# A state-space mixer kept channel-major: decay rows by DMA, diagonal and state products turned round, gate and squares channel-major

## The chip, the cores and the metric

The kernel runs on one core of one Trainium2 chip. The metric is the time of one execution on the device in microseconds; the time before is the median of three runs, 2385.97 us (2383.77 to 2386.37).

The engines are named as in the profile: PE multiplies matrices (PEld loads its weights), DVE, ACT and POOL work element by element, SP issues most DMAs. Each runs its own instructions in order and waits on semaphores. Operands lie in SBUF, PE writes to eight PSUM banks of 2 KB a partition.

## The reference

Layer norm and a mixer of Mamba-2 kind on 2 x 512 tokens of width 512, then layer norm and a mixture of experts, a block-sparse projection and the experts again, each added to x. The change touches the mixer alone. It has 8 groups of 16 heads with 64 channels, state size 128; the kernel takes chunks of 128 tokens where the reference has 32, for the same result.

```python
zxbcdt = hidden_states @ in_proj_w.T              # gate, x, B, C, dt
xBC = silu(causal_conv4(xBC) + conv_b)
dt = softplus(dt + dt_bias);  xs = x * dt;  Adt = -exp(A_log) * dt
A_cumsum = cumsum(Adt)                            # inside a chunk
L = exp(segment_sum(Ac))                          # exp(c_i - c_j), i >= j
Y_diag = einsum('bhcij,bcjhd->bcihd', (C @ B.T) * L, xs)
states = einsum('bckhn,bhck,bckhd->bchdn', B, exp(A_last - A_cumsum), xs)
# states are carried from chunk to chunk with exp(A_last)
Y_off = einsum('bckhn,bchdn,bhck->bckhd', C, states, exp(A_cumsum))
y = Y_diag + Y_off + D * x
y = y * silu(gate)
y = y * rsqrt(mean(y*y over the group's 1024 channels) + EPS) * norm_w
out = y @ out_proj_w.T
```

## The kernel before

After the first layer norm and the preparation (dt, the running sums c of A dt, and from them tables by token) a loop runs 8 times, once a group. Its body is one list of steps k, the same on every engine, unrolled: in step k each engine's code holds `if` blocks for all that is due in k. A unit of the recurrence is a pair of heads (128 channels) of one batch, four chunks of 128 tokens: 16 units u, unit u = (pair, batch).

- k 0 to 19: projection and convolution of B, C and the 8 tiles of x, for each batch. PE: 12 matmuls (weights and data are each split in a high and a low part, three products, helper `three`, L1479) into bank k % 3. ACT writes the last tap (L845), DVE adds the other three (L1164), ACT takes a tanh (L858), and DVE (k up to 9, L1173) or POOL (L641, L644) completes silu. x is channel-major here, [channel, token], in a ring of four buffers `cv`.
- k 20 to 35: 16 gate units of 12 matmuls: token-major, for tokens t and half of the channels. Tanh on ACT (L886), product on DVE (L1234), multiplied into Y on POOL (L654), squares summed on ACT (L900).
- k 36 to 43: 8 output tiles of 24 matmuls. Before each half, PE transposes y back to channel-major (`y_transpose`, L1526), ACT and DVE split it in parts `ah` (L915) and `al` (L1253). DVE adds the tile, times the reciprocal root rs8, to X (L1248). ACT's square root (L904) is in step NORM_AT = 38.

The recurrence of unit u runs beside these steps, at offsets `T_X, A_, B_, C_, D_ = 8, 9, 10, 11, 11`:

- k = u+8: PE transposes x to token-major (L1622) into bank TR.
- k = u+9: ACT copies it to Y (L808); DVE makes xs = x dt (L1225) and POOL xd = x dt decay (L610) from Y. PE spreads the two heads' rows c over the partitions with a matmul each (L1579: `pick_head` picks three bf16 parts from `rows`), ACT takes relu(c_j - c_i) (L874).
- k = u+10: ACT exponentiates (L815), DVE multiplies by G = C B (L1211). PE makes the state products of three chunks (L1594), DVE carries them along (L1147, L1152: S).
- k = u+11: PE makes the diagonal part in bank 6 (L1636) and the off part (L1650: weights C, columns S). DVE adds D x and the diagonal part (L1185) and scales the off part into yo (L1199).
- k = u+12: POOL adds yo to Y (L636).

State and off products share bank 7, so L1650 of unit u waits for the S of unit u+1. ACT and POOL also split the weights into `wh` (L826) and `wl` (L620), at the steps of `W_TICK`; SP loads them as the ring `raw` of four gets free.

## Time and profile before

| | |
|---|---|
| Median of 3 runs | 2385.97 us |
| Profiled execution | 2383.2 us, its span 2381.5 us |
| Mean granted TensorE clock | 0.975 of 2.4 GHz |
| PE, DVE, ACT, POOL busy | 92%, 68%, 51%, 44% of the span |
| HBM read and written | 142.42 MB and 25.95 MB |

"Span" is from the first instruction to the last. Groups of instructions are told apart by line, tiles and shape, and their "mean ns" is of one instruction; neighbours on one engine overlap by some 0.07 us, so that what follows starts a little before the end printed. A matmul's printed duration includes its way through the array: the distance of the starts is what it costs in a row of matmuls. fp32 matmuls have two records each. A wait stands in brackets behind the instruction that had to wait.

### The profile page before, as it was taken

The numbers are of one execution on the slowest core, as the hardware profiler recorded it, in microseconds if no ns is written. First come the engines' busy times: TensorE is split into PE (matmuls) and PEld (weight loads), VectorE is DVE, ScalarE is ACT, GpSimd is POOL, SyncE is SP. The second block draws the span as 40 slices with busy tenths as digits, with TensorE's granted clock in tenths as the row PEclk, the third lists the DMA queues.
The fourth block names the chain that finished last, engine by engine and source line by source line (L and its number), as shares of the span: only waits on it lengthen the run. The fifth ranks groups of instructions, "written<-read, shape, count | busy, mean of one in ns | idle before, by whom it ended". The sixth has DMA issues, their size and how long they took to land.

```text
span 2381.5 us, 40261 instructions
## 1 busy us (share of the span) xinstructions
PE 2201.0 (92%) x12416; PEld 1827.9 (77%) x12416; DVE 1630.3 (68%) x2891; ACT 1217.8 (51%) x2809; POOL 1051.3 (44%) x882
## 2 busy tenths in 40 slices
PE   3899999999999999999999999899989988989897
PEld 2778877887788778878887888788878867766775
DVE  6797389739973997499649965985598553157314
ACT  2576366636663665266537653764376422422341
POOL 3476047505750575057416731673276213430322
PEclk7999999999999999999999999999999999999999
DMA  1201011111011011101110111001101027950795
GB/s 60 100 28 36 20 44 32 32 35 32 28 32 40 27 32 33 40 23 37 41 29 26 36 37 31 31 28 37 35 28 27 18 97 250 391 168 36 261 398 159
DMA packets 87218, 171.26 MB, mean 72 GB/s; under 512 B 11464, under 2 KB 11464, under 8 KB 86984
## 3 DMA queue, kind: packets, MB, share of 16 engines
q1 hardware_dynamic: 78016, 140.35, 17.6%
q0 software_dynamic: 7520, 24.65, 3.2%
q10 hardware_dynamic: 1448, 3.41, 0.4%
q8 instruction: 114, 1.87, 0.3%
q14 instruction: 120, 0.98, 0.1%
HBM read 142.42 MB, written 25.95 MB: 71 GB/s over the span
## 4 chain that ended last, share of the span: by engine, by line
PE 55%; DVE 23%; issue 15%; POOL 3%; ACT 3%; DVEq 1%; another core or an unknown queue 1%; DMA 0%; ACTq 0%; POOLq 0%; SPq 0%
PE bank L1479 34%; PE bank L1783 5%; DVE mem L1211 5%; DVE cv L1164 4%; PE bank L1636 4%; DVE mem L1225 3%; PE bank L1795 2%; DVE Y L1185 2%; DVE mem L1152 2%; PE bank L1650 2%; POOL Y L654 1%; PE bank L1594 1%; PE bank L1526 1%; ACT mem L874 1%; DVE mem L1199 1%
## 5 line engine op out<-in xcount | busy, mean ns | idle before, releaser
L620 POOL TENSOR_TENSOR wl<-raw,wh 128x512 fp32r<-128x512 f32 x144 | 205.4, 1431 | 526.2 <-ACT wh L826 526.2
L874 ACT ACTIVATE mem<-bank,hp 128x128 f32<-128x128 f32 x1024 | 278.5, 384 | 134.3 <-PE bank L1636 134.3
L1479 PE MATMUL bank<-xh,wh 128*128 128x512 f32 x776 | 321.1, 414 | 17.9 <-POOL wl L620 11.0
L1479 PE MATMUL bank<-xh,wl 128*128 128x512 f32 x776 | 306.5, 395 | 0.0
L1479 PE MATMUL bank<-xl,wh 128*128 128x512 f32 x776 | 305.9, 394 | 0.0
L1164 DVE SCALAR_TENSOR_TENSOR cv<-bank,cpar,cv 128x511 f32<-128x511 f32 (+2 forms) x384 | 286.9, 747 | 20.7 <-ACT cv L845 11.7
L1636 PE MATMUL bank<-mem 128*128 128x64 f32 x2048 | 249.7, 275 | 18.3 <-DVE mem L1211 18.3
L1636 PEld LDWEIGHTS bank<-mem 128*128 128x128 f32 x2048 | 238.5, 192 | 32.1 <-DVE mem L1211 30.7
L1479 PE MATMUL bank<-wh,ah 128*128 128x512 f32 x576 | 239.4, 416 | 23.2 <-DVE al L1406 22.5
L1211 DVE TENSOR_TENSOR mem<-mem,quad 128x512 f32<-128x512 f32 x256 | 249.3, 1014 | 0.0
L1253 DVE TENSOR_TENSOR al<-bank,ah 128x512 fp32r<-128x512 f32 x128 | 88.6, 692 | 233.7 <-ACT ah L915 233.7
L1479 PE MATMUL bank<-wh,al 128*128 128x512 f32 x576 | 228.8, 397 | 0.0
L1479 PE MATMUL bank<-wl,ah 128*128 128x512 f32 x576 | 227.7, 395 | 0.0
L654 POOL TENSOR_TENSOR Y<-Y,gt 128x512 f32<-128x512 f32 x128 | 165.1, 1290 | 133.1 <-DVE gt L1234 133.1
L1479 PE MATMUL bank<-wh,xh 128*128 128x512 f32 x544 | 220.5, 405 | 1.4 <-DVE xl L1050 1.4
L1479 PE MATMUL bank<-wh,xl 128*128 128x512 f32 x544 | 212.9, 391 | 0.0
L1479 PE MATMUL bank<-wl,xh 128*128 128x512 f32 x544 | 211.8, 389 | 0.0
L915 ACT ACTIVATE ah<-bank 128x512 fp32r<-128x512 f32 x128 | 76.5, 597 | 259.9 <-PE bank L1526 259.9
L845 ACT ACTIVATE cv<-bank,cpar 128x512 f32<-128x512 f32 x128 | 100.1, 782 | 189.9 <-PE bank L1622 148.0
L1479 PEld LDWEIGHTS bank<-xh,wh 128*128 128x128 f32 x776 | 149.3, 192 | 49.0 <-issue 16.8
L636 POOL TENSOR_TENSOR Y<-Y,mem 128x384 f32<-128x384 f32 x128 | 162.0, 1266 | 48.3 <-DVE mem L1199 48.3
L610 POOL TENSOR_TENSOR mem<-Y,hp 128x384 f32<-128x384 f32 x128 | 115.3, 901 | 147.5 <-ACT Y L808 147.5
(218 smaller groups left out, 4670.5 us busy)
## 6 DMA issues: line engine op xcount, KB each, us to landing
mem<-wffn_d SPq DMA_DIRECT2D x62, 512.0 KB
raw<-wconv_d SPq DMA_DIRECT2D x80, 256.0 KB, 2.7
raw<-wgate_d SPq DMA_DIRECT2D x64, 256.0 KB, 2.6
raw<-wout_d SPq DMA_DIRECT2D x64, 256.0 KB, 2.6
slots_y<-quad SPq DMA_DIRECT2D x62, 256.0 KB
mem<-wffn_d SPq DMA_DIRECT2D x42, 256.0 KB
raw<-wffn_d SPq DMA_DIRECT2D x24, 256.0 KB
pick_head<-wffn_d SPq DMA_DIRECT2D x20, 256.0 KB
```

The costliest lines, as they stand in the source:

```text
L610: inc(pool.tensor_tensor(xd[:, u % 2, :, :].rearrange("p c (h d) -> p c h d", d=HD), Y[:, b * CH:(b + 1) * CH - 1, pair * P:(pair + 1) * P ...
L620: inc(pool.tensor_tensor(wl[:, W_SLOT[p], :], raw[:, R_SLOT[p], :], wh[:, W_SLOT[p], :], ALU.subtract), w_lo)
L636: inc(pool.tensor_tensor(dst, dst, yo[:, :, :], ALU.add), y_ok)
L654: inc(pool.tensor_tensor(dst, dst, gt[:, n % 2, :], ALU.mult), y_gated)
L845: inc(nc.scalar.activation(dst, bank[big_bank(k)][:, :], ACT.Identity, scale=cpar[:, tile, TAPS - 1:TAPS], bias=cpar[:, tile, TAPS:TAPS + ...
L874: last = nc.scalar.activation(L[:, n % 4, c * P:(c + 1) * P], bank[LB[h]][:, c * P:(c + 1) * P], ACT.Relu, scale=-1.0, bias=hp[:, b * CH + ...
L1164: last = STT(dst[:, s:SEQ], bank[big_bank(k)][:, 0:SEQ - s], cpar[:, tile, TAPS - 1 - s:TAPS - s], dst[:, s:SEQ], ALU.mult, ALU.add)
L1211: inc(TTn(L[:, n % 4, :], L[:, n % 4, :], G[:, b * CH:(b + 1) * CH, :].rearrange("p c i -> p (c i)"), ALU.mult), lg_ok)
L1253: inc(TTn(al[:, m, :, :], b4(TR), ah[:, m, :, :], ALU.subtract), y_lo)
L1479: got = mm(out, l, r, start=first and n == 0, stop=last and n == 2)
L1636: last = mm(b4(DG)[:, c, h * HD:(h + 1) * HD], L[:, (2 * u + h) % 4, c * P:(c + 1) * P], xs[:, u % 3, c, h * HD:(h + 1) * HD], start=True, ...
L1783: last = mm(bank[2 + tau % 2][:, a * P:(a + 1) * P], tgu[tau % GU_RING][:, a, kt * P:(kt + 1) * P], xT[tau % 2][:, kt, :], start=kt == 0, ...
```

## The change

Y is now channel-major from the convolution to the output.

- Rows: c of each head lies in DRAM (`c_rows`). For each unit SP loads, per head, one row of 512 into all 128 partitions of L (ring of 6) and of 384 into 64 partitions of E (ring of 3). ACT's relu and exponential work on L in place, another exponential on E. `pick_head`, the three bf16 parts and the row matmuls are gone.
- x: the convolution writes straight into Y. DVE makes xs from the transposed x in the bank, POOL xd from xs. ACT's copy is gone.
- Diagonal: the weights are xs (128 x 64 of one head), the columns L; the two heads write partitions 0 to 63 and 64 to 127 of banks 4 and 5 in turn. Off part: weights S, columns C, in a bank of its own.
- Gate: weights stationary, 8 channel tiles for each batch. Squares go to `sq`, POOL adds them to `acc`, and eight matmuls with a column of ones sum over the channels.
- Output: `ah` and `al` are made from Y; no transposes.

```diff
-        TR, LB, DG, SO = 3, (4, 5), 6, 7
+        TR, DG, ST, OF = 3, (4, 5), 6, 7
@@ SP, in the loop over k
+                def rows_in(u):
+                    pair, b = unit(u)
+                    if u >= LR // 2:
+                        now(sp, diag_mm, i, u - LR // 2 + 1)
...
+                    for h in range(2):
+                        n, a = 2 * u + h, 2 * pair + h
+                        sp.dma_start(L[n % LR], c_rows[i, a:a + 1, b * SEQ:(b + 1) * SEQ].to_broadcast([P, SEQ])
+                                     ).then_inc(row_in[n % LR], 16)
+                def scales_in(u):
+                    pair, b = unit(u)
+                    if u >= ER:
+                        now(sp, y_ok, i, u - ER + 1)
...
+                        sp.dma_start(E[h * HD:(h + 1) * HD, u % ER, :], c_rows[i, a:a + 1, b * SEQ + P:(b + 1) * SEQ]
+                                     .to_broadcast([HD, SEQ - P])).then_inc(e_in[u % ER], 16)
...
+                    for u in range(UNITS):
+                        if k == (u + 8 if u >= LR // 2 else u + 5):
+                            rows_in(u)
+                        if k == (u + 9 if u >= ER else u + 6):
+                            scales_in(u)
@@ POOL
-                        now(pool, tr_act, i, 2 + u + 1)
+                        now(pool, xs_ok, i, u + 1)
...
+                    n = k - 3 - NCONV
+                    if BATCH <= n < NGATE:
+                        now(pool, sq_ok, i, n + 1)
+                        if n >= 2 * BATCH:
+                            now(pool, ss_add, i, n - 2 * BATCH + 1)
+                        inc(pool.tensor_tensor(acc[:, n % 2, :], acc[:, n % 2, :], sq[:, n % 2, :], ALU.add), ss_add)
@@ ACT
-                        inc(nc.scalar.activation(Y[:, b * CH:(b + 1) * CH, pair * P:(pair + 1) * P], b4(TR),
-                                                 ACT.Copy, scale=0.5), tr_act)
...
+                        e_arrived(act, i, u)
+                        inc(nc.scalar.activation(E[:, u % ER, :], E[:, u % ER, :], ACT.Exp), e_ok)
...
-                        now(act, ss_ok, i, 1)
-                        inc(nc.scalar.activation(sd8[:, :], ssum[:, :], ACT.Sqrt, scale=1.0 / GW,
+                        now(act, ss_mm, i, 1)
+                        inc(nc.scalar.activation(sd8[:, :], bank[TR][:, 0:TT], ACT.Sqrt, scale=1.0 / GW,
@@ DVE
+                        dst = Y[:, pair, b * SEQ:(b + 1) * SEQ]
+                        inc(STT(dst, dst, dcol[:, pair:pair + 1], bank[DG[u % 2]][:, :], ALU.mult, ALU.add), ydiag_ok)
...
+                        inc(STT(E[:, u % ER, :], bank[OF][:, 0:(CH - 1) * P], 0.5, E[:, u % ER, :], ALU.mult,
+                                ALU.mult), off_ok)
@@ PE
-                            inc(mm(bank[LB[h]][:, :], pick_head[:, 2 * pair + h, :],
-                                   rows[:, b * SEQ:(b + 1) * SEQ], start=True, stop=True), row_mm)
...
-                        for h in range(2):
-                            for c in range(CH):
-                                last = mm(b4(DG)[:, c, h * HD:(h + 1) * HD],
-                                          L[:, (2 * u + h) % 4, c * P:(c + 1) * P],
-                                          xs[:, u % 3, c, h * HD:(h + 1) * HD], start=True, stop=True)
+                        for c in range(CH):
+                            for h in range(2):
+                                hs = slice(h * HD, (h + 1) * HD)
+                                last = mm(b4(DG[u % 2])[hs, c, :], xs[:, u % 3, c, hs],
+                                          L[(2 * u + h) % LR][:, c * P:(c + 1) * P], start=True, stop=True)
...
+                    if k == NORM_AT - 1:
+                        now(pe, xs_ok, i, UNITS)
+                        now(pe, ss_add, i, NGATE - BATCH)
+                        for t in range(TT):
+                            last = mm(bank[TR][:, t:t + 1], acc[:, t // CH, t % CH * P:(t % CH + 1) * P],
+                                      ones16[:, 0:1], start=True, stop=True)
+                        inc(last, ss_mm)
```

DVE, the end of step 12 and the start of step 13, in the order before (L1199 is the off part of unit 1, L1211 the decay of unit 2, L1225 the xs of unit 3, L1147 starts the S of unit 3):

```order
L1185 SCALAR_TENSOR_TENSOR Y<-Y,gpar,bank6 128x4x64 [waits xd_ok,diag_mm]
L1185 SCALAR_TENSOR_TENSOR Y<-Y,gpar,bank6 128x4x64
L1199 TENSOR_TENSOR mem<-bank7,hp 128x384 [waits y_ok,off_mm]
L1211 TENSOR_TENSOR mem<-mem,quad 128x512 [waits decay_ok] x2
L286 REGISTER_ALU
L1225 TENSOR_TENSOR mem<-Y,hp 128x512 [waits diag_mm,tr_act]
L286 REGISTER_ALU
L1147 COPY mem<-bank7 128x128 [waits off_mm,st_mm]
```

The same place now (L1209, L1215 and L1226 are units 1, 1 and 2 again, L1152 is the xs of unit 4):

```order
L1209 SCALAR_TENSOR_TENSOR Y<-Y,dcol,bank5 128x512 [waits diag_mm]
L1215 SCALAR_TENSOR_TENSOR E<-bank7,E 128x384 [waits e_ok,off_mm]
L1226 TENSOR_TENSOR cv<-cv,quad 128x512 [waits decay_ok] x2
L1152 TENSOR_TENSOR mem<-bank3,hpt 128x512 [waits diag_mm,tr_mm]
L296 REGISTER_ALU
L1167 COPY mem<-bank6 128x128 [waits off_mm,st_mm]
```

The xs at this place is that of a unit further on, so that it has moved forward by nearly a step, and it reads PE's bank 3: PE's transposes of the next unit wait for it, where they waited for ACT's copy.

ACT, around the tap of a convolution, now (L899 is the relu, L845 the exponential of L, L847 that of E, L857 a weight's high part, L874 the tap, L887 the tanh):

```order
L845 ACTIVATE mem<-mem 128x512 [waits fall_ok]
L296 REGISTER_ALU
L845 ACTIVATE mem<-mem 128x512 [waits fall_ok]
L254 REGISTER_ALU
L847 ACTIVATE E<-E 128x384 [waits e_in1]
L338 ISA
L857 ACTIVATE wh<-raw 128x512 [waits big_mm,raw_in0]
L296 REGISTER_ALU
L874 ACTIVATE Y<-bank2,cpar 128x512 [waits big_mm]
```

L847 is new and waits for a DMA; the tap behind it does not start before.

ACT in step 38 before, and now (in `sd8` is the root; `ah` behind it is that of output tile 2):

```order
L904 ACT_TABLE_LOAD
L904 ACTIVATE sd8<-ssum,eps_c 128x8 [waits ss_ok]
L286 REGISTER_ALU
L286 REGISTER_ALU [waits tr_mm]
L915 ACTIVATE ah<-bank3 128x512 [waits out_half]
```

```order
L927 ACT_TABLE_LOAD
L927 ACTIVATE sd8<-bank3,eps_c 128x8 [waits ss_mm]
L296 REGISTER_ALU [waits y_gated]
L937 ACTIVATE ah<-Y 128x512 [waits out_half]
```

The root waited for DVE's sum of ACT's squares; now it waits for PE's eight matmuls, which stand on PE behind the second output tile:

```order
L1475 MATMUL bank1<-wh,al 128x512
L296 ISA [waits xs_ok]
L1629 MATMUL bank3<-ones16,cv 128x1 [waits ss_add]
L1629 MATMUL bank3<-ones16,cv 128x1 x7
L1475 MATMUL bank2<-wh,ah 128x512 [waits y_lo,gate_ok]
L1475 MATMUL bank2<-wl,ah 128x512
```

## Rows read from the trace of the kernel before

**Rows 1.** page, part 1: busy us and share of the span

```profile
PE 2201.0 (92%) x12416; PEld 1827.9 (77%) x12416; DVE 1630.3 (68%) x2891; ACT 1217.8 (51%) x2809; POOL 1051.3 (44%) x882
```

**Rows 2.** windows of two stages: us; busy us (instructions) by engine; clock, DMA share, GB/s

```profile
566.50:648.30 81.80, 73.07 (x465) 61.78 (x464) 79.74 (x144) 56.16 (x144) 61.68 (x49) 0.98 0.08 25
648.30:688.10 39.80, 39.64 (x264) 34.78 (x265) 32.38 (x71) 25.76 (x73) 23.73 (x21) 1.00 0.09 25
```

**Rows 3.** DVE timeline: start us, us, engine, line, operation

```profile
575.25 0.28 DVE L1147 COPY mem<-bank 128x128 f32<-128x128 f32 x1
...
647.12 0.28 DVE L1147 COPY mem<-bank 128x128 f32<-128x128 f32 x1
```

**Rows 4.** groups, DVE, steps 10 to 19: busy us, mean ns; idle before

```profile
L1211 DVE TENSOR_TENSOR mem<-mem,quad 128x512 f32<-128x512 f32 x20 | 21.4, 1109 | 0.0
L1225 DVE TENSOR_TENSOR mem<-Y,hp 128x512 f32<-128x512 f32 x11 | 14.5, 1314 | 0.0
...
L1199 DVE TENSOR_TENSOR mem<-bank,hp 128x384 f32<-128x384 f32 x9 | 5.0, 552 | 0.0
```

**Rows 5.** groups, DVE, steps 20 to 26

```profile
L1211 DVE TENSOR_TENSOR mem<-mem,quad 128x512 f32<-128x512 f32 x12 | 10.6, 923 | 0.0
...
L1234 DVE SCALAR_TENSOR_TENSOR gt<-gt,bank 128x512 f32<-128x512 f32 x7 | 4.7, 675 | 0.0
L1199 DVE TENSOR_TENSOR mem<-bank,hp 128x384 f32<-128x384 f32 x7 | 3.9, 554 | 0.4 <-PE bank L1650 0.2
L1225 DVE TENSOR_TENSOR mem<-Y,hp 128x512 f32<-128x512 f32 x5 | 3.4, 678 | 0.0
```

**Rows 6.** groups, ACT, steps 10 to 19

```profile
L815 ACT ACTIVATE mem<-mem 128x512 f32<-128x512 f32 x22 | 13.3, 690 | 0.0
L845 ACT ACTIVATE cv<-bank,cpar 128x512 f32<-128x512 f32 x10 | 7.8, 783 | 15.3 <-PE bank L1622 15.2
```

**Rows 7.** groups, POOL, steps 10 to 19

```profile
L636 POOL TENSOR_TENSOR Y<-Y,mem 128x384 f32<-128x384 f32 x9 | 12.6, 1400 | 1.8 <-DVE mem L1199 1.8
L620 POOL TENSOR_TENSOR wl<-raw,wh 128x512 fp32r<-128x512 f32 x8 | 12.6, 1577 | 3.4 <-ACT wh L826 3.4
L610 POOL TENSOR_TENSOR mem<-Y,hp 128x384 f32<-128x384 f32 x11 | 10.1, 918 | 9.0 <-ACT Y L808 9.0
```

**Rows 8.** PE timeline, one unit in step 24

```profile
672.32 0.60 PE L1579 MATMUL bank<-rows,pick_head 128*128 128x512 bf16 x2
672.76 0.83 PE L1594 MATMUL bank<-mem,quad 128*128 128x128 f32 x6
673.42 1.90 PE L1636 MATMUL bank<-mem 128*128 128x64 f32 x16
675.16 0.89 PE L1650 MATMUL bank<-mem,quad 128*128 128x128 f32 x6
```

**Rows 9.** PE timeline in the output projection

```profile
754.51 0.60 PE L1526 MATMUL bank<-ident,Y 128*128 128x128 f32 x4
...
757.70 0.60 PE L1526 MATMUL bank<-ident,Y 128*128 128x128 f32 x4
...
759.76 0.39 PE L1479 MATMUL bank<-wl,ah 128*128 128x512 f32 x1
...
760.21 0.39 PE L1479 MATMUL bank<-wh,ah 128*128 128x512 f32 x1
```

**Rows 10.** page, parts 3 and 6: a DMA queue; issues, KB each, us to landing

```profile
q1 hardware_dynamic: 78016, 140.35, 17.6%
...
raw<-wconv_d SPq DMA_DIRECT2D x80, 256.0 KB, 2.7
...
X<-x_d SPq DMA_DIRECT2D x4, 512.0 KB, 5.4
```

**Rows 11.** timeline: ACT's square root and DVE's first X

```profile
721.93 0.30 ACT L904 ACTIVATE sd<-ssum,eps_c 128x8 f32<-128x8 f32 x1
...
722.61 0.75 DVE L1248 SCALAR_TENSOR_TENSOR X<-bank,rs,X 128x512 f32<-128x512 f32 x1
```

379 lines of the change are left out of this document (159 added, 220 removed).

## The prediction

> **What bounds the kernel now.** I read the busy shares first, then one pass of the group loop cut into stages, then for each stage the timeline of the engine that never rests. PE is busy 92% of the span and DVE 68% [rows 1]; this reads as one bound, but the stages differ. Two stages of one pass (of 8) are shown [rows 2]: steps k 10 to 19 (81.8 us), where a projection with its convolution runs beside the recurrence of another unit, and steps 20 to 26 (39.8 us) with gate and recurrence. In the first DVE is busy 79.7 of 81.8 us and PE 73.1; nine steps run from the L1147 at 575.25 to that at 647.12 [rows 3], 7.99 us each. There DVE is the pace. In the second PE is busy 39.6 of 39.8. In the gates alone and in the output projection PE is the pace too: one 512-column matmul starts 0.226 us behind the other [rows 9].
>
> **The change, part by part.** The sum is made for one of the 8 passes and against the profiled execution: span 2381.5 us, 2383.2 as run, 0.1% from the median of the runs (2385.97), which I neglect.
>
> *Steps 10 to 19 (DVE).* L1225, which scales x into xs, reads Y in SBUF and takes 1.31 us here [rows 4], 0.68 in steps 20 to 26, where POOL does less [rows 5]. L1199, which reads a bank, has 0.55 in either stage [rows 4, 5]: what reads a bank keeps its time beside POOL. After, xs comes from the bank: 0.69 by L1234 on the same 512 elements, so 0.62 less a step. The two halves of the D term become one instruction (a little shorter, not counted), off gets a third operand, as L1234 has it, for no more. L1211 keeps its work (1.11 each, two a step). Without POOL the pair would be 1.36, by the 0.68 of L1225, the same form; with POOL at it throughout 2.6, by the 1.31. The step gets shorter and POOL's work does not, so I take no change, and the bounds are -0.9 and +0.4 a step. By the sum the step is 7.4 us: **-6 a pass** (bounds -15 and -2).
>
> *Decay rows.* PE's two broadcast matmuls (0.44 us a unit [rows 8]) go; two DMAs of 256 KB and two of 96 KB a unit come. On ACT the copy of x (512 elements) goes and the exponential of E (384) comes; the Relu keeps its shape. The new waits are ACT's. That for E of unit k-10 stands in front of the tap of conv k: behind it are queued wh, the tap, the tanh and the next Relus, and DVE's taps wait for the tap. E is requested only when POOL has added unit k-13. From the start of a step on DVE: xs 0.6, POOL's xd 0.92, wl 1.58 in six of the ten steps, the add 1.40 [rows 7]; the request leaves at 2.9 or at 4.5 us. Then the exponential (0.5 for 384 elements, by the 0.69 that L815 takes for 512), wh (0.6) and the tap (0.7, of the 0.78 of L845 [rows 6]) must be over by 7.4 + 1.8, since xs and S (which I put at 1.2) stand before the taps. This leaves 2.9 us for the landing where there is a wl, and 5.1 elsewhere. 256 KB of weights land in 2.7 us, four loads of 512 KB issued together in 5.4 [rows 10]; the unit's 704 KB, of which the rows leave a microsecond ahead, I put at 3.3. So 0.2 us in six steps would do; I charge 0.2 in six: **+1.2 a pass** (bounds 0 and +25). The bandwidth suffices: 78016 packets took 17.6% of 16 engines [rows 10], and 384 more a unit, 49152 in all, add 11%.
>
> *Steps 20 to 26 (PE and DVE in turn).* Six steps of 6.5 us. PE loses 0.44 a step, but gains a wait: its transposes of x need xs of the unit before, which DVE does behind off, two L1211 and the gate. From the end of one off to the next: DVE 0.55 + 1.85 + 0.6 + 0.6 [rows 5], PE transposes 0.40 (by the 0.35 to 0.48 of the y transposes), diagonal 1.74, off 0.66 by L1594, handovers 0.1: 6.5, as before. I take **-0.5 a pass** (bounds -5 and +5). The diagonal changes its shape. Now 16 records with 128x128 weights and 64 columns take 1.74 us, 0.109 each, and L1594 with 128x128 weights and 128 columns 0.66 for six, 0.110 each [rows 8]. After, the weights have 64 columns and 128 stream; the larger of the two is still 128, so 0.109 again.
>
> The Trainium skill (TensorEngine Tiling (Array Packing), "Key Properties") says that different tiles run LdWeights and Matmul in parallel, and that a change of the tiling mode drains the array. By the first the diagonal would take half; by the second each unit pays two drains. No row here shows either; rivals 2 and 3 hold what they would do.
>
> *Gates and output.* The 16 groups of y transposes go. From one L1526 to the next it is 3.19 us, of which 12 matmuls are 2.71 [rows 9]; 16 times 0.48 is -7.7. Added: eight matmuls with one column for the sums of squares, 16 records bound by their 128 weight columns at 0.11: +1.85 with the change of form. And the norm moves onto the path: they stand on PE behind output tile 1, ACT's square root waits for them, and behind the square root stand the ah copies of tile 2, behind the reciprocal and X of tile 0 on DVE the al of tile 2. PE stands from the last of the eight until al(2,0): from the start of sd to that of X 0.68 us [rows 11], X 0.65, al 0.69, handovers 0.15: +2.15. Before, ssum came from squares that no PE work followed, and this cost nothing. The table load stands ahead of the wait in the order, so it stays hidden; else 1.28 more. ah(1,0) stands behind the last square, +0.3. Sum **-3.4 a pass** (bounds -7.5 and +2). POOL gets 14 additions of 512 a pass, about 1.3 us each: in the gate steps 2.6 of PE's 2.71. They just fit, and if each took 1.45 instead, ten steps would be 0.2 longer.
>
> *The rest.* Step 9 loses its rows: -0.4. The seam between passes and the preparation I leave at 0; what follows the mixer is unchanged.
>
> Sum: -0.4 - 6 + 1.2 - 0.5 - 3.4 = -9.1 a pass, times 8 = -73: 2383 - 73 = **2310 us** (-3%).
>
> **Rivals.**
> 1. *Slower: the ring of E paces steps 10 to 19.* With a landing of D the step is 3.45 + D + 0.5 + 0.3 + 0.7 - 1.8. It decides from D = 5.3, where a step of 8.4 uses up the 4.3 gained elsewhere. With 6 (the four loads took 5.4, and here 128 partitions read one and the same row in DRAM, which no row shows) the step is 9.15: +11.6 - 4.3 = +7.3 a pass, 2383 + 58 = 2441. Against it: a weight load lands in 2.7, and E is the smaller.
> 2. *The column halves overlap.* The two heads of a unit write partitions 0 to 63 and 64 to 127. Side by side the diagonal is 0.87 and the chain of steps 20 to 26 is 5.6: -0.87, six steps, 8 passes: -41, 2269. A drain, if it is the 0.17 us by which a matmul outlasts the start of the next (0.39 to 0.226), twice a unit, gives back 16. In steps 10 to 19 DVE hides both.
> 3. *The diagonal gets slower or DVE's gain is eaten.* Half of the weight time (0.055) no longer behind the columns: 0.164 a record, +0.88 a unit, +42, 2352. Or POOL, denser now, stretches L1211, and with the wl steps the stage stays at 8.0: +38, 2348.
> 4. *DVE and POOL fall apart in time* (pair of L1211 at 1.4): step 6.7, a further -48, 2262.
>
> **Chances.** Forecast 0.50 (own range 2285 to 2335); rival 1 0.12; rivals 2 and 4 together 0.20 (2240 to 2285); rival 3 0.18 (2335 to 2385). A measurement of this kernel tells 0.2%, about 5 us, from no change. Faster by more: 0.50 + 0.20 + 0.15 = 0.85; within it 0.03; slower 0.12. The range of 2240 to 2375 leaves out rival 1 and the tips of 3 and 4.
>
> **What would show it.** Right: xs at 0.69 in every step; DVE without waits and 7.2 to 7.6 us a step in steps 10 to 19; ACT waiting for E's DMA in the steps with wl alone; 2.7 us for each half tile of the output, with one gap of about 2 us on PE in each pass, between the eight small matmuls and tile 2; 1.75 us for the diagonal. Wrong: ACT waiting for row or E transfers in most steps (rival 1), DVE's taps waiting for ACT, gates that take more than 2.73 us each with POOL never idle, or a diagonal far from 1.75.

## The result, and the profile after

| | median of the runs | ratio to before, 95% |
|---|---|---|
| before | 2384.87 us (2378.16 to 2386.37) | |
| after | 2348.89 us (2343.39 to 2352.1) | 0.9852 [0.9823, 0.9882] |

The change gains 1.5%, where 3% was forecast: 35 of 73 us. The profiled execution has a span of 2350.0 us, as run 2352.1. The first part of its page:

```profile
PE 2056.1 (87%) x11776; PEld 1686.0 (72%) x11776; DVE 1587.6 (68%) x2766; ACT 1232.1 (52%) x2680; POOL 1166.2 (50%) x987
```

Against [rows 1] PE has lost 145 us of work and five points of its share: it waits more. To see where, each pass is cut at the copy that starts a unit's S on DVE (L1167 now, L1147 before [rows 3]) and at the first and last matmul of the output. Mean of seven passes, us, computed from the starts in the timelines:

| stretch | before | after | change | forecast |
|---|---|---|---|---|
| steps 10 to 19 (nine units' S) | 70.87 | 62.89 | -8.0 | -4.8 |
| steps 19 to 25 (six units' S) | 40.74 | 41.47 | +0.7 | -0.5 |
| last S to first output matmul | 33.07 | 31.03 | -2.0 | } |
| output, first to last matmul | 50.47 | 55.01 | +4.5 | } -3.4 together |
| to the next pass's first S | 37.47 | 37.73 | +0.3 | -0.4 |
| pass | 232.62 | 228.12 | -4.5 | -9.1 |

The third pass in windows (steps 10 to 19, steps 20 to 26 as in [rows 2], the output, and the two slow places in it; us, then busy us and instructions of PE, PEld, DVE, ACT, POOL, then PE's clock as a share of full, DMA share, GB/s):

```profile
561.00:631.50 70.50, 60.24 (x427) 50.10 (x425) 67.77 (x129) 55.53 (x140) 51.67 (x45) 0.98 0.38 119
631.50:671.30 39.80, 34.95 (x267) 28.91 (x267) 36.00 (x65) 28.06 (x72) 28.72 (x25) 1.00 0.38 108
696.50:750.50 54.00, 48.52 (x208) 39.76 (x207) 19.02 (x25) 15.79 (x25) 9.77 (x9) 0.94 0.07 21
700.90:706.50 5.60, 3.82 (x10) 2.98 (x11) 3.24 (x3) 1.32 (x3) 5.35 (x4) 0.72 0.38 109
717.00:720.50 3.50, 3.50 (x10) 2.76 (x9) 0.73 (x2) 0.00 (x0) 0.00 (x0) 0.51 0.00 0
```

In [rows 2] PE was busy 39.64 of 39.80 us in the second stage; now it is 34.95. In the last row PE is busy throughout at a clock of 0.51: the lower of its two levels, 1.2 GHz (the upper is 2.4).

The output on PE (start, us, operation, idle time before it and what ended it):

```profile
699.00 0.39 PE L1475 MATMUL bank<-wh,al 128*128 128x512 f32 x1
702.68 0.50 PE L1475 MATMUL bank<-wh,ah 128*128 128x512 f32 x1 [3.30 <-DVE wl L1139]
...
703.96 0.63 PE L1475 MATMUL bank<-wl,ah 128*128 128x512 f32 x1
704.38 0.63 PE L1475 MATMUL bank<-wh,al 128*128 128x512 f32 x1
...
712.59 1.84 PE L1629 MATMUL bank<-ones,cv 128*128 128x1 f32 x16
716.61 0.47 PE L1475 MATMUL bank<-wh,ah 128*128 128x512 f32 x1 [2.18 <-DVE al L1249]
```

The second wait, 2.18 us, is the forecast one. The first, 3.30, is not in the forecast at all; it stands in the middle of the first output tile, behind 12 of its 24 matmuls. Behind both the matmuls start 0.425 us apart and not 0.226 as in [rows 9]. Over seven passes the time lost in these wider starts adds up to 3.9 us a pass, about 2.0 behind each wait. With the two waits, the 1.84 of the eight small matmuls and 43.4 for 192 matmuls at 0.227 (the last one's start), this makes 54.6 of the 55.0.

GpSimd and DVE ahead of the first wait:

```profile
691.52 1.75 POOL L692 TENSOR_TENSOR Y<-Y,gt 128x512 f32<-128x512 f32 x1
693.21 1.75 POOL L699 TENSOR_TENSOR cv<-cv,sq 128x512 f32<-128x512 f32 x1
694.92 1.75 POOL L692 TENSOR_TENSOR Y<-Y,gt 128x512 f32<-128x512 f32 x1
696.63 1.29 POOL L699 TENSOR_TENSOR cv<-cv,sq 128x512 f32<-128x512 f32 x1
697.88 1.29 POOL L692 TENSOR_TENSOR Y<-Y,gt 128x512 f32<-128x512 f32 x1
```

```profile
697.41 0.69 DVE L1233 SCALAR_TENSOR_TENSOR gt<-gt,bank 128x512 f32<-128x512 f32 x1 [1.30 <-ACT gt L911]
699.87 1.09 DVE L1249 TENSOR_TENSOR al<-Y,ah 128x512 fp32r<-128x512 f32 x1 [1.77 <-ACT ah L937]
700.88 1.75 DVE L1139 SCALAR_TENSOR_TENSOR wl<-raw,gpar,wh 128x512 fp32r<-128x512 f32 x1
```

And GpSimd's groups in the gates alone (671.3 to 696.5; busy, mean ns, idle before):

```profile
L692 POOL TENSOR_TENSOR Y<-Y,gt 128x512 f32<-128x512 f32 x9 | 14.3, 1591 | 1.2 <-DVE gt L1233 1.2
L699 POOL TENSOR_TENSOR cv<-cv,sq 128x512 f32<-128x512 f32 x8 | 11.2, 1404 | 0.0
```

A gate product and an addition take POOL 3.0 us in the mean, in steps of 2.72, and it hardly rests. The product of 697.88 is the one that rows of the first output tile need; the ah and al follow it, and in DVE's queue the last piece of the output weight stands behind that al. From the end of that product (699.17) follow ah to 699.84, al to 700.96, wl to 702.63, and PE at 702.68.

Step 20, the seam between convolution and gates, in the fourth pass; ACT, then POOL:

```profile
858.18 0.52 ACT L847 ACTIVATE E<-E 128x384 f32<-128x384 f32 x1 [2.32 <-DMA E<-c_rows]
858.61 0.61 ACT L857 ACTIVATE wh<-raw 128x512 fp32r<-128x512 f32 x1
859.13 0.61 ACT L887 ACTIVATE gt<-Y 128x512 f32<-128x512 f32 x1
859.65 2.44 ACT L899 ACTIVATE cv<-cv,hpt 128x128 f32<-128x128 f32 x8
864.96 0.60 ACT L911 ACTIVATE gt<-bank 128x512 f32<-128x512 f32 x1 [2.87 <-POOL Y L683]
```

```profile
859.31 1.29 POOL L659 TENSOR_TENSOR wl<-raw,wh 128x512 fp32r<-128x512 f32 x1 [0.63 <-ACT wh L857]
860.54 1.03 POOL L675 TENSOR_TENSOR Y<-Y,E 128x384 f32<-128x384 f32 x1
861.51 1.75 POOL L681 TENSOR_TENSOR gt<-Y,gt 128x512 f32<-128x512 f32 x1
863.34 1.59 POOL L683 TENSOR_TENSOR Y<-Y,gt 128x512 f32<-128x512 f32 x1
```

ACT waits 2.32 us for the transfer of E; wh and the tanh of the last convolution come late by it; POOL works in order through wl, the decayed sum and the convolution's two operations; the first gate's tanh waits for these. The step takes 8.7 us (6.2 before), the next 7.6 (6.8 before).

### The profile page after: what moved, and what is told of

Same layout as the page of the kernel before. It is cut to its first block, busy times and chain, and to the rows that moved or that the text cites. A ratio compares the mean times of both kernels' runs of the same rounds, so it can differ in the third digit from the quotient of the medians.

```text
span 2350.0 us, 39600 instructions
## 1 busy us (share of the span) xinstructions
PE 2056.1 (87%) x11776; PEld 1686.0 (72%) x11776; DVE 1587.6 (68%) x2766; ACT 1232.1 (52%) x2680; POOL 1166.2 (50%) x987
## 3 DMA queue, kind: packets, MB, share of 16 engines
q8 instruction: 106, 1.74, 0.3%
## 4 chain that ended last, share of the span: by engine, by line
PE 33%; issue 28%; POOL 20%; DVE 13%; ACT 2%; DMA 2%; another core or an unknown queue 1%; POOLq 0%; SPq 0%; DVEq 0%; ACTq 0%
PE bank L1475 21%; POOL Y L692 5%; PE bank L1758 5%; POOL gt L681 4%; POOL cv L699 4%; POOL Y L675 3%; PE bank L1770 2%; POOL wl L659 2%; DVE mem L1226 2%; DVE Y L1184 1%; POOL mem L650 1%; PE bank L1745 1%; DVE mem L1152 1%; PE bank L1608 1%
## 5 line engine op out<-in xcount | busy, mean ns | idle before, releaser
L1475 PE MATMUL bank<-xh,wh 128*128 128x512 f32 x1288 | 525.0, 408 | 16.8 <-POOL wl L659 10.6
L1475 PE MATMUL bank<-xh,wl 128*128 128x512 f32 x1288 | 505.0, 392 | 0.0
L1475 PE MATMUL bank<-xl,wh 128*128 128x512 f32 x1288 | 504.2, 391 | 0.0
L1184 DVE SCALAR_TENSOR_TENSOR Y<-bank,cpar,Y 128x511 f32<-128x511 f32 (+2 forms) x384 | 287.0, 747 | 20.5 <-ACT Y L874 10.4
L1475 PEld LDWEIGHTS bank<-xh,wl 128*128 128x128 f32 x1288 | 243.2, 189 | 53.4
L1475 PEld LDWEIGHTS bank<-xl,wh 128*128 128x128 f32 x1288 | 244.7, 190 | 45.3 <-issue 0.5
L650 POOL TENSOR_TENSOR mem<-mem,hpt 128x384 f32<-128x384 f32 x128 | 106.7, 834 | 263.6 <-DVE mem L1152 263.6
L899 ACT ACTIVATE mem<-mem,hpt 128x128 f32<-128x128 f32 x704 | 214.9, 390 | 12.3 <-DMA mem<-c_rows 12.3
L692 POOL TENSOR_TENSOR Y<-Y,gt 128x512 f32<-128x512 f32 x128 | 195.1, 1524 | 19.6 <-DVE gt L1233 19.6
L1475 PEld LDWEIGHTS bank<-wh,ah 128*128 128x128 f32 x576 | 117.4, 204 | 104.9 <-DVE wl L1139 30.0
L1226 DVE TENSOR_TENSOR mem<-mem,quad 128x512 f32<-128x512 f32 x176 | 183.2, 1080 | 0.0
L699 POOL TENSOR_TENSOR cv<-cv,sq 128x512 f32<-128x512 f32 x112 | 154.5, 1385 | 0.0
```

What stands on the lines that cost most here:

```text
L650: inc(pool.tensor_tensor(xd[:, u % 2, :, :].rearrange("p c (h d) -> p c h d", d=HD), xs[:, u % 3, 0:CH - 1, :].rearrange("p c (h d) -> p c ...
L692: inc(pool.tensor_tensor(dst, dst, gt[:, n % 2, :], ALU.mult), y_gated)
L699: inc(pool.tensor_tensor(acc[:, n % 2, :], acc[:, n % 2, :], sq[:, n % 2, :], ALU.add), ss_add)
L899: last = nc.scalar.activation(L[n % LR][:, c * P:(c + 1) * P], L[n % LR][:, c * P:(c + 1) * P], ACT.Relu, scale=-1.0, bias=hp[:, b * CH + ...
L1184: last = STT(dst[:, s:SEQ], bank[big_bank(k)][:, 0:SEQ - s], cpar[:, tile, TAPS - 1 - s:TAPS - s], dst[:, s:SEQ], ALU.mult, ALU.add)
L1226: inc(TTn(L[n % LR], L[n % LR], G[:, b * CH:(b + 1) * CH, :].rearrange("p c i -> p (c i)"), ALU.mult), lg_ok)
```

## The experiments

"Equals" below is the ratio to the runs of before on the same chip, times 2384.87; the changed kernel equals 2350 on this scale. Each ratio is known to about 0.2%, so two runs differ surely from about 8 us on. "Pass", "steps 19 to 25" and "output" are the means of the table above, from one profiled execution each. Part of what the ratios show lies outside the passes: the stretch behind the mixer's last output, whose code no run's edit changes, took 446 to 460 us in these executions (460 in the changed kernel's, 448 in e8's). What an edit gains in the mixer is therefore read more surely from the pass, times 8.

| run | ratio, 95% | equals | pass | steps 19 to 25 | output |
|---|---|---|---|---|---|
| changed kernel | 0.9852 [0.9823, 0.9882] | 2350 | 228.1 | 41.5 | 55.0 |
| e1 | 0.9711 [0.9686, 0.9736] | 2316 | 223.9 | 41.5 | 51.1 |
| e2 | 0.9684 [0.9662, 0.9705] | 2310 | 223.8 | 41.5 | 50.7 |
| e3 | 0.9761 [0.974, 0.9782] | 2328 | 225.9 | 41.6 | 52.9 |
| e4 | 0.9657 [0.9633, 0.9681] | 2303 | 222.6 | 41.5 | 49.8 |
| e5 | 0.9686 [0.9668, 0.9704] | 2310 | 224.1 | 42.0 | 50.4 |
| e6 | 0.9823 [0.9802, 0.9844] | 2343 | 227.4 | 40.7 | 54.3 |
| e7 | 0.9694 [0.9676, 0.9711] | 2312 | 223.9 | 37.8 | 54.5 |
| e8 | 0.9774 [0.9756, 0.9792] | 2331 | 226.7 | 40.4 | 54.7 |
| e9 | 0.9893 [0.9875, 0.9911] | 2359 | 229.6 | 42.4 | 55.2 |
| e10 | 0.9596 [0.9581, 0.9611] | 2289 | 220.8 | 40.0 | 49.2 |
| e11 | 0.9585 [0.9572, 0.9598] | 2286 | 221.2 | 39.9 | 50.8 |
| e12 | 0.9621 [0.9608, 0.9635] | 2294 | 221.8 | 40.1 | 49.3 |
| e13 | 0.9873 [0.9855, 0.9891] | 2355 | 228.7 | 41.5 | 55.5 |
| e14 | 0.9918 [0.9904, 0.9932] | 2365 | 230.4 | 44.1 | 54.6 |
| e15 | 0.9656 [0.9641, 0.9671] | 2303 | 222.5 | 42.3 | 48.7 |
| e16 | 0.9655 [0.9641, 0.967] | 2303 | 222.5 | 42.0 | 48.8 |
| e17 | 0.9781 [0.9761, 0.98] | 2333 | 226.4 | 40.3 | 54.5 |
| e18 | 0.9558 [0.9539, 0.9577] | 2279 | 219.6 | 39.3 | 48.8 |

The steps 10 to 19 stayed at 62.8 to 63.1 in all of them.

**e1: without the additions.**

```diff
-                        inc(pool.tensor_tensor(acc[:, n % 2, :], acc[:, n % 2, :], sq[:, n % 2, :], ALU.add), ss_add)
-                        now(pe, ss_add, i, NGATE - BATCH)
+                        now(pe, sq_ok, i, NGATE)
```

> GpSimd's 14 additions of squares a pass are left out: the sums of squares come from tiles 0's squares alone (the second factor's values are other than the reference's), TensorE waits for the last square instead. Theory A (the additions were priced wrongly; in the changed kernel's trace GpSimd needs 1.74 for a gate product and 1.29 for an addition, some 3.0 us in a step of 2.72, so gated pieces fall behind, VectorE's low part of the output weight starts late, TensorE stands 3.4 us before the first output group, and then its matmuls start 0.425 instead of 0.227 us apart for some 3 us, 1.6 us more): both go, 5.0 us x 8 = 40 less than the changed kernel, 2309 us. Theory B (the stall has another cause, as VectorE's own queue or the weights' transfer): within 5 us of the changed kernel. If the gap goes and the clock stays low (the clock falls for another reason): 3.4 x 8 = 27 less, 2322.

34 us less, where theory A had 40. The additions cost 4 us a pass, nearly all of it in the output, but they are not the whole stall. Its row in the third pass:

```profile
689.84 0.50 PE L1469 MATMUL bank<-wh,ah 128*128 128x512 f32 x1 [1.36 <-DVE wl L1133]
```

1.36 us are left, and behind them the matmuls keep their 0.227 in all eight passes.

**e2: root a step later.**

```diff
-                    if k == NORM_AT:
+                    if k == NORM_AT + 1:
-                    t = k - NORM_AT
+                    t = k - NORM_AT - 1
```

> The root on ScalarE, the reciprocal and the eight residual sums on VectorE come one step later in their queues (step 39 instead of 38); TensorE's eight products with ones stay where they are, and nothing is left out. Theory A (the wait of 2.18 us for root, reciprocal, first residual and low part before the third output group, forecast as 2.15, and the lowered clock behind it, 1.65): both go, 3.8 x 8 = 31 less than the changed kernel, 2318 us. Theory B (the clock does not hang on the gap): the gap alone, 2.2 x 8 = 17 less, 2331. Theory C (the residual sums, one step later, hold a bank: a new wait before the fourth group takes the gap's place): within 5 us of the changed kernel.

40 us less, 35 of it in the passes: theory A (31), theory C refuted. The wait of 2.18 is gone, and the output is 4.3 us shorter, twice the wait itself. The eight small matmuls stay, and with no wait behind them the matmuls that follow start 0.23 us apart in all eight passes. The third pass has one slow place now and not two (first window 0.63, second 1.00):

```profile
692.60:697.20 4.60, 4.59 (x13) 3.67 (x14) 1.80 (x1) 1.15 (x2) 3.56 (x3) 0.63 0.61 187
697.20:706.00 8.80, 8.80 (x49) 7.54 (x48) 3.00 (x5) 3.45 (x5) 0.00 (x0) 1.00 0.06 23
```

**e3: additions on VectorE, and e4: both.**

```diff
-                        inc(pool.tensor_tensor(acc[:, n % 2, :], acc[:, n % 2, :], sq[:, n % 2, :], ALU.add), ss_add)
+                        inc(TTn(acc[:, n % 2, :], acc[:, n % 2, :], sq[:, n % 2, :], ALU.add), ss_add)
```

> The 14 additions of squares stand on VectorE, ahead of the gate's product of each step, not on GpSimd; nothing is left out. Theory A (GpSimd's 3.0 us a step is what makes the stall): like the run without additions, if VectorE takes them at about 0.7 us each beside its gate product and weight's low part: 2309 to 2315 us. Rival (VectorE's gate product comes late then, since in steps 25 and 26 it still has the heads' work, and banks come free late): a gain under 15 us, 2335 or more.

> Both edits: additions on VectorE, root and residual sums a step later; nothing is left out. Theory A (two gaps, each with a lowered clock behind it, add up): 40 + 31 less than the changed kernel, 2278 to 2290 us, and the mixer passes' granted clock back at 0.98 or more. Rival (the two share their cost, or the clock stays): 2300 or more.

e3 gains 22 us, between the two: the stall in the third pass is 2.79 us. VectorE's low parts now stand behind its own additions, which is the likely reason; no run took that apart. e4 gains 47 us, not 71: the rival, though most of it is there.

**e5: the stall's order.** PE waits for the last weight piece ahead of its last use alone; ACT and DVE split that piece ahead of ah(0,1) and al(0,1); and the root as in e2.

```diff
+                                if t == 0 and m == 1 and j == 3:
+                                    piece_split(pe, i, PIECES - 1)
...
+                    if k == NCONV + NGATE - 1:
+                        for p in range(PIECES - 1, PIECES):
```

> Besides the root one step later, the last piece of the output weight is taken out of the stall's way: TensorE waits for it only ahead of the last 3 of the first group's 24 matmuls (not ahead of 12), and ScalarE and VectorE split it ahead of the last piece's rows of the first group, not behind; nothing is left out, and the additions stay on GpSimd. Theory A (without the additions 1.36 us of the stall of 3.30 stayed in the third pass, and with them on VectorE 2.79: so what holds TensorE is the weight's low part standing behind the first group's low part in VectorE's queue, itself behind GpSimd's last products): the stall goes from 3.36 to under 1, and with it half of the lowered clock: 2.4 + 1 us x 8 = 27 less than with the root moved alone (2309), 2282 us. Rival (GpSimd's backlog itself, through the rows of the second half, is what is waited for, whatever the order): the stall stays over 2.5 and the time within 8 us of 2309.

Like e2: the rival's time, with a wait as long as before, and now al ends it:

```profile
692.69 0.77 PE L1493 MATMUL bank<-wh,ah 128*128 128x512 f32 x1 [3.38 <-DVE al L1267]
```

The weight was not taken out of the way, though. DVE in the same pass:

```profile
689.16 1.71 DVE L1262 SCALAR_TENSOR_TENSOR wl<-raw,gpar,wh 128x512 fp32r<-128x512 f32 x1 [1.14 <-ACT wh L938]
690.80 1.75 DVE L1267 TENSOR_TENSOR al<-Y,ah 128x512 fp32r<-128x512 f32 x1
```

The ah that this al needs was ready at 689.77, and al starts only when wl ends: wl, which itself waited for ACT's wh until 689.13, has moved from behind al to ahead of it in the same queue. Both kernels do one wl and one al between POOL's late product (end 689.10 here, 699.17 in the changed kernel) and PE's restart, and the stretch is 3.59 and 3.51 us. So e5 does not tell the weight's share of the stall from that of POOL's lateness.

**e6: one head after the other.**

```diff
-                        for c in range(CH):
-                            for h in range(2):
+                        for h in range(2):
+                            for c in range(CH):
```

> Of the changed kernel, the diagonal product's 16 matmuls of 128x64 go through the four chunks of the one head and then of the other, instead of the two heads in turn; the same matmuls, nothing left out. In the changed kernel's trace 16 take 1.02 us (1.74 before the change, with 64 rows of weights a head). Theory A (neighbours in different column halves overlap, and this overlap was hidden): the 16 take about 1.7 us again, TensorE's wait for VectorE's x piece shrinks by as much in steps 10 to 19, and the time is within 8 us of the changed kernel (2349). Rival B (no overlap of halves; the 16 are short for another reason): 1.02 stays. Rival C (TensorE is on the path there): 1.7 us and 16 x 0.7 x 8 = 90 us more at most, over 20 at least.

Theory A in the mechanism. The same 16 records with the heads in turn (changed kernel), and head after head (e6); the start of L1622 is their end:

```profile
568.29 1.09 PE L1608 MATMUL bank<-mem 128*64 128x128 f32 x16
569.32 0.94 PE L1622 MATMUL bank<-quad,mem 128*128 128x128 f32 x6
```

```profile
568.55 1.58 PE L1608 MATMUL bank<-mem 128*64 128x128 f32 x16
570.06 0.94 PE L1622 MATMUL bank<-quad,mem 128*128 128x128 f32 x6
```

1.03 against 1.51 us, and 1.74 in [rows 8]. The time is 7 us less, which the intervals don't tell from none. It is a balance and not "no effect": steps 20 and 21 got 1.0 and 0.9 us shorter (why, no run shows), step 22 got 0.7 and step 19 0.3 longer, and the stretch from the last S to the output 0.6 longer.

**e7: GpSimd without four low parts.**

```diff
+                            if k >= NCONV:
+                                pool.sem_inc(per[w_lo][0], 1)
+                                continue
```

> Of the changed kernel, GpSimd's low part of the four gate weights of steps 20 to 23 is left out (TensorE multiplies with what stood in those tiles, so the low products' values are other than the reference's). GpSimd then has a product, a sum and a gate product in these steps, some 3.4 us of 6.8 and not 5. Theory A (in steps 20 to 24 VectorE's decay products slow down from 0.65 to 1.1 us and more while GpSimd works, and x pieces for TensorE come late by it; step 6.79 where 6.5 was forecast): the step falls to 6.5 or less in those four, 1.2 us a pass, 10 us less, 2339. Rival (that time hangs on ScalarE or TensorE): within 4 us of the changed kernel.

38 us less (34 in the passes), over three times theory A. Steps 19 to 25 fall from 41.5 to 37.8. DVE in step 21 of the third pass, in the changed kernel and here:

```profile
641.39 0.75 DVE L1209 SCALAR_TENSOR_TENSOR Y<-Y,dcol,bank 128x512 f32<-128x512 f32 x1 [0.57 <-PE bank L1608]
642.25 0.56 DVE L1215 SCALAR_TENSOR_TENSOR E<-bank,E 128x384 f32<-128x384 f32 x1
642.72 2.41 DVE L1226 TENSOR_TENSOR cv<-cv,quad 128x512 f32<-128x512 f32 x2
645.05 0.67 DVE L1233 SCALAR_TENSOR_TENSOR gt<-gt,bank 128x512 f32<-128x512 f32 x1
```

```profile
629.73 0.75 DVE L1212 SCALAR_TENSOR_TENSOR Y<-Y,dcol,bank 128x512 f32<-128x512 f32 x1 [0.57 <-PE bank L1611]
630.58 0.56 DVE L1218 SCALAR_TENSOR_TENSOR E<-bank,E 128x384 f32<-128x384 f32 x1
631.06 1.28 DVE L1229 TENSOR_TENSOR cv<-cv,quad 128x512 f32<-128x512 f32 x2
632.26 0.68 DVE L1236 SCALAR_TENSOR_TENSOR gt<-gt,bank 128x512 f32<-128x512 f32 x1
```

In the first POOL's gate product runs from 642.68 to 643.98, beside the pair; in the second it had ended at 631.08. The pair differs by 1.13 us, all else by nothing, and from this pair to the next it is 5.8 us and not 6.7; in the 5.8 PE has no idle time left. The third pass is a strong case: in the mean the pair of step 21 fell from 1.6 to 1.3 and that of step 22 from 2.1 to 1.3. And step 20 gave 1.2 us too, where the pair stayed at 3.0: a second cause, which e8 and e17 find.

**e8: E's exponential behind the tanh.**

```diff
+                        inc(nc.scalar.activation(gt[:, kc % 2, :], src, ACT.Tanh, scale=0.5), conv_th)
...
+                        e_arrived(act, i, u)
+                        inc(nc.scalar.activation(E[:, u % ER, :], E[:, u % ER, :], ACT.Exp), e_ok)
```

> Of the changed kernel, ScalarE's exponential of the broadcast decay row E comes behind the bias tap and the tanh of its step instead of ahead; nothing left out. Its wait for that transfer is 153.7 us over the run (88 times, up to 3.0). Theory A (that wait is idle time off the path: VectorE's taps wait for ScalarE 10.4 us in all): 0 to 8 us less than the changed kernel. Rival (the ring of E paces steps 10 to 19): 15 us less or more, the step of 7.11 us falls under 6.9. A rise would show that VectorE's off-diagonal product waits for E instead.

19 us less, the size that the rival gave; 12 of it are in the passes. The steps 10 to 19 did not move (62.8), so both the "0 to 8" and the rival's place were wrong: 9 of the 12 are in steps 20 (8.7 to 8.0) and 21 (7.6 to 7.2).

**e9: gate product first on GpSimd.** The block of L692 stands at the head of the step, otherwise unchanged.

```diff
+                    kg = k - 1
+                    if NCONV <= kg < NCONV + NGATE:
...
                     u = k - (B_ - 1)
```

> Of the changed kernel, GpSimd's gate product stands at the head of its step (ahead of the state scaling, the weight's low part and the decayed sum), not behind them; the same work, nothing left out. Without the low part of four weights the step of 21 fell from 6.7 to 5.8 us, where GpSimd's gate product ended as VectorE's pair of decay products (L1226) began, and the pair took 1.28 instead of 2.41. Theory A (it is the overlap of just these two that costs): the gate product falls into VectorE's product out of PSUM, the pair shrinks to 1.3 to 1.9 us in steps 21 to 24, 2 to 3 us a pass: 15 to 25 less than the changed kernel (2349), 2324 to 2334. Theory B (any GpSimd work there does it, and the amount alone counts): the low part or the decayed sum now lies beside the pair, which stays near 2.4, and the time within 8 us.

9 us more, at the edge of what can be told. The pair did shrink (steps 21 and 22: 1.28 and 1.56 us in the mean, from 1.59 and 2.16; step 24: 1.41 from 2.84), and the time did not. What stands behind the gate product now, the decayed sum, is what E's next load waits for: ACT's wait for E rose from 153.7 to 167.5 us. In step 24 of the third pass the pair took 1.40 us and DVE then waited for the gate's tanh, which stands on ACT behind a wait of 1.24 us for E and one of 0.83 for a row of L; the step got 0.9 us longer in the mean:

```profile
669.05 0.69 DVE L1233 SCALAR_TENSOR_TENSOR gt<-gt,bank 128x512 f32<-128x512 f32 x1 [2.14 <-ACT gt L911]
```

**e10 to e12: combinations.** e10 is e2, e5, e8 and e9, and POOL adds the squares of the first half of the tokens, DVE those of the second; e11 has all additions on DVE; e12 is e10 with e6's order.

```diff
-                    if BATCH <= n < NGATE:
+                    if BATCH <= n < NGATE and n % 2 == 0:
```

> All together, nothing left out: gate product first on GpSimd, E's exponential behind the tanh, root and residual sums a step later, the last weight piece split and waited for late, and the additions of squares split: those of the first half of the tokens on GpSimd, of the second on VectorE. Theory A (GpSimd's 3.0 us in a step of 2.72 falls to 2.2 to 2.4, its backlog goes, and the stall ahead of the first output group with it; the gains of moving the root, 40, the exponential, 19, and the overlap, 15 to 25, add up with 15 to 25 for the stall): 2250 to 2270 us. Rival (each gain was the same wait seen from another side, as the stall of 3.4 us stayed when only its order was changed): 2285 to 2305.

> As the run before, with all additions on VectorE. Theory A (GpSimd then never lags, and VectorE has room for 0.7 us a step from step 27 on; but in steps 25 and 26 it has none): within 8 us of the split version. Rival (VectorE becomes late with the output weights' low parts, the stall of 2.79 stays): 10 to 25 above it.

> The split version with the diagonal's matmuls head after head instead of in turn (16 in 1.7 us instead of 1.0, if that depends on neighbours in different column halves). Theory A (with VectorE's pair shorter, TensorE is the path in steps 20 to 26, and the 0.7 us a unit are seen there, six or seven units a pass): 30 to 40 above the split version. Rival (VectorE remains the path there, hiding it as in the changed kernel): within 8 us.

61, 64 and 56 us less than the changed kernel: e10 near its rival, e11 as its theory A. The stall is down to 2.4 us (e10), not gone. With the slower diagonal (e12) it is 6 us more, which the intervals hardly tell from none (8 by the passes), and not 30 to 40. Steps 19 to 25 stay at 40.1: its pairs in steps 21 to 24 are at 1.28 to 1.30, probably because they come later than POOL's work, and make up for the 0.5 us more on PE.

**e13: PE kept busy in its waits.**

```diff
+                            if (t, m) in ((0, 1), (2, 0)):
+                                for _ in range(13 if t == 0 else 8):
+                                    mm(bank[DG[0]][:, 0:P], ident[:, :], ident[:, :], start=True, stop=True)
```

> The changed kernel, with 13 products of 128x128 with the identity (26 records, 2.9 us at 0.11 each) on TensorE into a bank that is free, ahead of the wait for the second half of the first output group, and 8 (1.8 us) ahead of the wait for the third group; all else as it was. They fill 2.9 of the 3.3 us and 1.8 of the 2.2 us in which TensorE waits. Theory A (the granted clock falls because TensorE has stood still): the stalls end when they did, but the matmuls behind them start 0.227 apart at once: 3.1 us a pass, 25 less than the changed kernel (2349), 2324 us. Theory B (clock falls for another reason, or a matmul more is a cost anywhere): within 5 us, or more than the changed kernel.

Nothing gained, which is the time that theory B gave, but the reason is in the trace: the first 13 stood behind the wait for the weight piece, so they ran after the stall (700.89 to 705.24, 4.35 us) and not in it. The second eight stood right:

```profile
713.73 1.84 PE L1634 MATMUL bank<-ones,cv 128*128 128x1 f32 x16
715.43 2.03 PE L1551 MATMUL bank<-ident 128*128 128x128 f32 x16
717.66 0.50 PE L1475 MATMUL bank<-wh,ah 128*128 128x512 f32 x1 [0.19 <-DVE al L1249]
717.99 0.39 PE L1475 MATMUL bank<-wl,ah 128*128 128x512 f32 x1
718.22 0.39 PE L1475 MATMUL bank<-wh,al 128*128 128x512 f32 x1
```

Behind a wait of the same length that is filled, the starts soon are 0.23 us apart. Behind the second wait this held in all eight passes, where the changed kernel lost 1.6 us or more in each: theory A for the mechanism. The 4.35 us of misplaced filling gave the gain back.

**e14: last convolution first on GpSimd.** The block of L681 and L683, for step 20 alone, stands ahead of wl and the decayed sum.

```diff
+                    if kc == NCONV - 1:
+                        now(pool, conv_th, i, kc + 1)
```

> Of the changed kernel, in step 20 alone GpSimd does the product and the sum of the last convolution ahead of the weight's low part and the decayed sum, not behind them; nothing left out. Theory A (the first gate's tanh waits for that sum, and with it the product, the x piece and TensorE's transposes): the step of 20 falls from 8.7 to 6.5 us: 2.2 x 8 = 18 less than the changed kernel, 2331, and 6 more where the clock stays up behind the shorter gap. Theory B (contention between GpSimd and VectorE makes the step long whatever the order): within 6 us of the changed kernel.

Step 20 fell (8.7 to 7.1 us), and the whole got 15 us longer, as neither theory had it: steps 21 and 22 rose from 7.6 and 6.2 to 9.8 and 8.4. ACT in step 21:

```profile
875.36 0.53 ACT L855 ACTIVATE E<-E 128x384 f32<-128x384 f32 x1 [4.98 <-DMA E<-c_rows]
```

The decayed sum ended at 871.35, and E, whose load waits for it, came 4.0 us later.

**e15, e16: combinations with it.** e10 with e14's edit, without (e15) and with (e16) e9's.

> The earlier combination (root and residual sums a step later, last weight piece split and waited for late, additions of squares split between GpSimd and VectorE, E's exponential behind the tanh) with the last convolution's product and sum first in step 20, and the gate product where the changed kernel has it. Nothing left out. Theory A (step 20 gives 1.5 us more, and the gate product in its old place 1.0 us): 2285 - 20 = 2265. Rival (E's exponential behind the tanh has given step 20's time already: it stood at 8.0 there): 2278 or more.

> As the run before, with GpSimd's gate product at the head of its step. In the combination the pairs of decay products in steps 22 to 24 took 1.4 to 1.8 us with it, 2.2 to 2.8 in the changed kernel. Theory A (once GpSimd has less to do, the gate product first costs nothing and takes the overlap away): 5 to 15 below the run before. Rival (it holds up the state scaling, and what waits for it, as alone): 5 to 10 above.

Both 14 us above e10, which neither theory A had: e14's loss again (steps 21 and 22 are 9.4 and 7.8 in e15), and the gate product's place makes no difference.

**e17: a fourth buffer of E, asked for a step earlier, and e18: with the rest (e15).**

```diff
-        LR, ER = 6, 3
+        LR, ER = 6, 4
-                        if k == (u + 9 if u >= ER else u + 6):
+                        if k == (u + 8 if u >= ER else u + 6):
```

> The changed kernel with four buffers of E instead of three, and E of a unit asked for one step earlier in SyncE's queue (behind the unit's own rows, not behind the next unit's); nothing left out. Theory A (the ring of E sets the time in steps 19 to 25: ScalarE waits there for the transfer, and the weight's high part, the tanh and the exponentials come late behind it): ScalarE's wait for E falls from 153.7 us to under 40, the steps 19 to 25 from 41.5 to 39 or less, 2349 - 20 = 2329 or less. Theory B (GpSimd's and VectorE's overlap alone makes them long): the wait goes, the steps stay at 41, the time within 8 us.

> The combination of e15 (root a step later, last weight piece split and waited for late, additions split between two engines, E's exponential behind the tanh, last convolution first in step 20) with four buffers of E. Nothing left out. Theory A (e15 lost in steps 21 and 22 what it won in step 20, 9.4 and 8.0 us there, by waiting for E): these two fall to 6.5 and 6.2, 4.5 us a pass: 2300 - 36 = 2264, the shortest of all. Rival (E was not what held them): 2285 or more.

ACT's wait for E over the run, in the changed kernel and in e17 (busy, mean ns, then idle before it):

```profile
L847 ACT ACTIVATE E<-E 128x384 f32<-128x384 f32 x128 | 66.5, 519 | 153.7 <-DMA E<-c_rows 153.7
```

```profile
L847 ACT ACTIVATE E<-E 128x384 f32<-128x384 f32 x128 | 65.4, 511 | 0.0
```

The wait is gone, and 17 us with it (14 in the passes, of which 9 in steps 20 and 21: 8.0 and 7.2, as in e8). Part of it went elsewhere: ACT's wait for the rows of L (L899) rose from 16.7 to 59.0 us. e17's 40.3 us for steps 19 to 25 lie between the two theories: the ring and the earlier request, which this run does not tell apart, are 1.2 us a pass. What the rest hangs on, e7 shows in part; a wider ring for L is not tried. e18, with the last convolution first, no longer loses in step 21 (6.8) what it wins in step 20 (7.0); its step 22 is 6.7, and the whole is 15 us above what theory A said. At 2279 it is the shortest of all, 4.4% below before and 3.0% below the change as made.

## Why the prediction was off

The forecast was -73 us; -35 came. The 2349 us are the number of rival 3 (2348) by chance: it let the diagonal get slower or steps 10 to 19 stay at 8.0 us, and the diagonal fell to 1.03 and these steps to 7.0. By the forecast's own steps, us a pass:

- **Steps 10 to 19: -8.0, forecast -6 and +1.2.** Right in the mechanism, as far as the traces tell (no run undid it): xs takes 0.68 in every step. The step is 7.0 (forecast 7.4). Before it was 7.87 in the mean, where the forecast started from the third pass's 7.99 [rows 3]; of the 0.89 that went xs is 0.68, the D term 0.10 and the pair 0.17, with S 0.06 longer. The pair L1226 took 1.28 to 1.46 in four of the nine steps, 2.2 to 3.0 in the others (in part what rival 4 had, 1.4 throughout). The 1.2 for late E loads was not paid here: with the ring widened (e17) the stage stays at 62.8.
- **Steps 20 to 26: +0.7, forecast -0.5. A term mis-sized, and a wait not seen.** The chain took the pair at 1.85, the mean of [rows 5]. It was 2.4 in the mean of steps 20 to 24, where POOL's work lies beside it. With a free pair the step is 5.8 us (e7), and that is PE's own work with no idle time in it, the diagonal at 1.03 (rival 2 had 5.6 for the chain); so the column halves do overlap, as that rival had it, and DVE hid the gain. And E's ring, rival 1, given 0.12 for steps 10 to 19 and absent there, costs at the seam of step 20, where POOL has both the convolution and a wl: 1.1 to 1.2 (e8, e17).
- **Gates and output: +2.5, forecast -3.4. The step that failed.** The transposes went and the small matmuls (1.84) and the wait behind the root (2.18) came as computed. Two terms were missing. First, "they just fit": POOL's product and addition were put at 2.6 of 2.71 us. They take 3.0, because each slows to 1.75 while DVE works on weights, al and the like. The backlog ends in a wait of 3.3 us in the middle of the first output tile; without additions 1.36 stay (e1), which DVE's wl ends there too. Second, the clock: behind each of the two waits PE ran at 1.2 GHz for a while, 3.9 us a pass. e1, e2 and e13 show that it hangs on PE's waits: with the wait shortened to 1.36, gone, or filled it does not come. A wait was costed at its length; the one of 2.18, which was forecast, cost 4.3 (e2).
- **Step 9 and seams: +0.3, forecast -0.4.** Small, the cause stays open.

Together the missing 3.3 and 3.9 are 7.2 us of the output; steps 19 to 25 add 1.2 and the seams 0.7. The steps 10 to 19 gave 3.2 back. 1.3 more came ahead of the output, where the last two units' diagonals got 0.7 shorter each, less a new wait of 0.46 (e6 takes 0.6 of it away), and from the 0.3 put for ah(1,0), which was not paid. This makes the 4.6 between -9.1 and -4.5.

Two sums of the rivals do not come out of their own terms. Rival 1 has 3.45 us ahead of the landing; xs 0.6, xd 0.92, wl in six of ten steps 0.95 and the add 1.40 make 3.9. Rival 4's step of 6.7 against 7.4 is -56 and not -48. Neither touches the forecast.

The view that would have warned was there: [rows 7] have POOL's sum of 384 elements at 1.40 and its wl at 1.58 in the dense stage. An addition of 512 at 1.3 was the one choice on which "just fit" hung; the text priced the other case, 1.45 each, at 0.2 in ten steps, and left it out of the sum.

What stays open: why the stall of e10 is still 2.4 us (the chain from the last gates through tanh, POOL, ah and al is in the trace, but no run cut it); how much of the 1.36 of e1 is the order of the last weight piece; how much of e7's 3.7 us is the pair and how much the earlier request for E (e17 has 1.2 for ring and request).

## What to carry to other kernels

Cost a new wait of TensorE at its length and then what the clock takes behind it, and look for an order in which the queue in front of the waiting engine still has matmuls: moving the root one step (e2) took 35 us out of the passes, as much as the whole change brought. Work put on an engine that "just fits" must be costed at the slow duration that it shows beside its neighbour. And when an edit that should remove a wait gains nothing, read what the waiting engine now waits for before dropping it: in e5 the work had only changed places in one queue, and in e14, and in part in e9, a load was asked for later. e14's edit lost 15 us alone and is part of the best version, where the ring behind it has a buffer more.
